# Two cross-attention layers: the transposed probabilities of each pair of heads leave PSUM head by head, half by ScalarE and half by VectorE, ahead of the row maxima

## What is computed

```python
def _gqa_forward(hidden_state, encoder_hidden_state, encoder_attention_mask, Wq, bq, Wk, bk, Wv, bv, Wo, bo, gamma, beta):
    ...
    scores = jnp.einsum('bkgld,bksd->bkgls', q, k) * scale
    scores = scores + encoder_attention_mask[:, :, None, :, :]
    attn = jax.nn.softmax(scores, axis=-1)
    out = jnp.einsum('bkgls,bksd->bkgld', attn, v)
...
def _L1_xattn_ref(hidden_states, audio_kv, audio_attention_mask, Wq, Wk, Wv, Wo, ln_gamma, ln_beta, gate):
    ...
    a = _layer_norm(audio_kv, ln_gamma, ln_beta)
    ...
    attn = jax.nn.softmax(scores, axis=-1)
    out = jnp.einsum('bhts,bhsd->bhtd', attn, V)
    out = out.transpose(0, 2, 1, 3).reshape(B, Tt, D)
    out = out @ Wo.T
    return hidden_states + jnp.tanh(gate) * out
```

## Time and profile before

| what | value |
|---|---|
| median of 3 runs | 1238.89 us (1238.04 to 1239.21) |
| the profiled execution's own time | 1238.88 us |
| its span, first to last instruction | 1237.1 us |
| PE busy | 1163.7 us (94%) |
| DVE busy | 810.3 us (65%) |
| ACT busy | 749.9 us (61%) |
| POOL busy | 259.9 us (21%) |
| granted TensorE clock, mean | 0.991 |

### The profile page before, as it was taken

The page is one execution under the profiler, slowest core; times in us unless marked ns, Lnnn a source line. Parts: engine busy times, 40 slices in busy tenths (PEclk is TensorE's granted clock), DMA queues, the critical chain, the costliest instruction groups (busy, mean ns, idle before and its releaser), DMA issues.

```text
span 1237.1 us, 32215 instructions
## 1 busy us (share of the span) xinstructions
PE 1163.7 (94%) x9987; PEld 942.3 (76%) x9987; DVE 810.3 (65%) x2387; ACT 749.9 (61%) x2163; POOL 259.9 (21%) x280
## 2 busy tenths in 40 slices
PE   4899999999999999999999999999999999999997
PEld 4678787777878777787877778777787877778785
DVE  4465667667576775757667575766757576676734
ACT  3374756747475674747567474856747476574744
POOL 2042213121131312113121121312112131212210
PEclk9799999999999999999999999999999999999999
DMA  7674536447353654736365472635637263563600
GB/s 240 180 175 99 143 88 157 117 100 189 81 156 76 147 134 91 193 75 156 86 135 146 88 195 68 163 88 123 158 88 181 71 162 98 110 167 81 149 11 8
DMA packets 77821, 153.77 MB, mean 124 GB/s; under 512 B 10384, under 2 KB 47056, under 8 KB 77152
## 3 DMA queue, kind: packets, MB, share of 16 engines
q1 hardware_dynamic: 77792, 153.40, 50.6%
HBM read 113.72 MB, written 39.65 MB: 124 GB/s over the span
## 4 chain that ended last, share of the span: by engine, by line
PE 72%; issue 12%; DVE 9%; ACT 4%; DMA 1%; DVEq 1%; POOL 1%; ACTq 0%; SPq 0%; POOLq 0%
PE PJ L365 17%; PE TP L416 13%; PE SCO L402 6%; PE OA L436 5%; PE SCO L460 5%; PE SCO L681 5%; PE PJ L378 5%; PE PJ L468 4%; DVE SCO L819 3%; PE SCO L406 3%; PE SCO L365 2%; ACT PR L1049 2%; DVE PT L829 2%; DVE MN L819 1%; PE SCO L666 1%
## 5 line engine op out<-in xcount | busy, mean ns | idle before, releaser
L1049 ACT ACTIVATE PR<-SCO,MN 100x361 f32<-100x361 f32 x768 | 424.8, 564 | 154.3 <-DVE MN L819 151.1
L819 DVE CUSTOM_DVE_ANT_0 SCO<-SCO,MK 100x361 f32<-100x361 f32 x768 | 402.3, 549 | 148.1 <-PE SCO L402 102.3
L416 PE MATMUL TP<-ident,PR 100*128 100x100 f32 x2304 | 268.4, 252 | 22.3 <-DVE PT L829 19.7
L416 PEld LDWEIGHTS TP<-ident,PR 100*128 100x128 f32 x2304 | 226.9, 141 | 80.5 <-DVE PT L829 27.1
L1060 ACT ACTIVATE PT<-TP 121x600 f32<-121x600 f32 x256 | 173.0, 676 | 77.0 <-PE TP L416 76.6
L402 PE MATMUL SCO<-K0S,Q0S 128*100 128x362 f32 x512 | 164.1, 375 | 19.7 <-ACT PR L1049 17.5
L1049 ACT ACTIVATION_READ_ACCUMULATOR PR<-SCO,MN 100x1 f32 x768 | 158.2, 206 | 0.0
L829 DVE COPY PT<-TP 121x600 f32<-121x600 f32 x128 | 100.0, 781 | 52.1 <-PE TP L416 50.1
L819 DVE DVE_READ_ACCUMULATOR2_ANT MN<- 100x1 f32 x768 | 108.7, 141 | 0.0
L402 PEld LDWEIGHTS SCO<-K0S,Q0S 128*100 128x100 f32 x512 | 75.4, 166 | 43.1 <-ACT PR L1049 38.2
L406 PE MATMUL SCO<-K1S,Q1S 128*100 128x362 f32 x256 | 96.6, 387 | 8.1 <-ACT Q1S L1171 5.0
(11 more groups left out here) (142 smaller groups left out, 1827.7 us busy)
## 6 DMA issues: line engine op xcount, KB each, us to landing
K1S<-k_scr SPq DMA_DIRECT2D x128, 364.0 KB, 6.1
k_scr<-K1HL SPq DMA_DIRECT2D x64, 364.0 KB, 2.5
Q0S<-q_scr SPq DMA_DIRECT2D x128, 100.0 KB, 3.9
K0S<-k_scr SPq DMA_DIRECT2D x64, 182.0 KB, 4.8
AT<-ctx_cols SPq DMA_DIRECT2D x16, 722.0 KB, 9.3
V<-ctx_rows SPq DMA_DIRECT2D x16, 484.0 KB
q_scr<-QHL SPq DMA_DIRECT2D x16, 400.0 KB, 2.5
k_scr<-K1HL SPq DMA_DIRECT2D x32, 182.0 KB, 3.1
```

What stands on the lines that cost most here:

```text
L416: last = pe.transpose(TP[:, k % 2, c * T:(c + 1) * T], PR[0:T, k % NPR, c * SP:c * SP + P], ident[0:T, 0:T])
L819: dve.tensor_tensor_reduce(out=bank, in0=bank, in1=mask[0:T, :], scale=scale, scalar=3.4e38, op0=ALU.add, op1=ALU.min, accum_out=MN[0:T, k ...
L1049: act.activation(PR[0:T, k % NPR, 0:S], SCO[0:T, k % 3, 0:S], ACT.Exp, bias=MN[0:T, k:k + 1], scale=-1.0, accum_out=SM[0:T, k:k + 1]).then ...
```

## The change

Every pair is now copied by both engines at once: ACT copies the bank of its first head (121 x 300), DVE the bank of its second head (121 x 300). PE increments `pt_mm` after each head, so ACT can start after three transposes. PE waits for ACT's copy of the pair before ahead of the first head's transposes, and for DVE's ahead of the second head's. The exps wait for their slot of PR by heads and no longer by pairs. On DVE the copy of pair p-3 now stands ahead of both row maxima of step p in every step of L0 and L1. Pairs 14 and 15 are copied on DVE around the sums of the batch's second unit of 16 heads (`repeat_sums(b, 1)`).

```diff
             def transpose_probs(b, p):
                 pe.wait_ge(prob, NH * b + 2 * p + 2)
-                if p > 0:
-                    pe.wait_ge(*copied_out(b, p - 1))
-                elif not isinstance(b, int) or b > 0:
-                    pe.wait_ge(*copied_out(b - 1, NPAIR - 1))
+                wait_from(pe, pt_act, NPAIR * b + p)
                 for k in (2 * p, 2 * p + 1):
+                    if k % 2 == 1:
+                        wait_from(pe, pt_dve, NPAIR * b + p)
                     for c in range(SC):
                         last = pe.transpose(TP[:, k % 2, c * T:(c + 1) * T], PR[0:T, k % NPR, c * SP:c * SP + P],
                                             ident[0:T, 0:T])
-                last.then_inc(pt_mm, 1)
+                    last.then_inc(pt_mm, 1)
...
             def probs_out(b, p):
-                dve.wait_ge(pt_mm, NPAIR * b + p + 1)
+                dve.wait_ge(pt_mm, NH * b + 2 * p + 2)
...
-                dve.tensor_copy(PT[0:SP, h % 2, 2 * (p % 4):2 * (p % 4) + 2, :], TP[0:SP, :, 0:SC * T]).then_inc(pt_dve, 1)
+                dve.tensor_copy(PT[0:SP, h % 2, 2 * (p % 4) + 1, :], TP[0:SP, 1, 0:SC * T]).then_inc(pt_dve, 1)
...
                 for p in range(L0P):
-                    if p % 4 == 0 and (p > 0 or not first):
-                        if p > 0:
-                            probs_out(b, p - 3)
-                        else:
-                            probs_out(b - 1, NPAIR - 3)
-                    elif p == 2 and not first:
-                        probs_out(b - 1, NPAIR - 1)
+                    if p >= 3:
+                        probs_out(b, p - 3)
+                    elif not first:
+                        probs_out(b - 1, NPAIR - 3 + p)
...
+                probs_out(b, 14)
                 repeat_sums(b, 1)
+                probs_out(b, 15)
...
                 for p in range(L0P, NPAIR):
+                    if p >= 19:
+                        probs_out(b, p - 3)
                     shift(b, 2 * p)
-                    if p in (20, 22):
-                        probs_out(b, p - 3)
-                    elif more and p == 18:
+                    if more and p == 18:
...
             def exps(b, k):
                 act.wait_ge(shifted, NH * b + k + 1)
-                wait_from(act, pt_mm, NPAIR * b + k // 2 - 2)
+                wait_from(act, pt_mm, NH * b + k - 5)
...
             def probs_out(b, p):
-                act.wait_ge(pt_mm, NPAIR * b + p + 1)
+                act.wait_ge(pt_mm, NH * b + 2 * p + 1)
...
-                act.activation(PT[0:SP, h % 2, 2 * (p % 4):2 * (p % 4) + 2, :], TP[0:SP, :, 0:SC * T], ACT.Copy).then_inc(pt_act, 1)
+                act.activation(PT[0:SP, h % 2, 2 * (p % 4), :], TP[0:SP, 0, 0:SC * T], ACT.Copy).then_inc(pt_act, 1)
...
-                    if p >= 3 and (p - 3) % 4 != 1:
+                    if p >= 3:
                         probs_out(b, p - 3)
-                    elif p == 1 and not first:
-                        probs_out(b - 1, NPAIR - 2)
+                    elif not first:
+                        probs_out(b - 1, NPAIR - 3 + p)
...
                     exps(b, 2 * p - 2)
-                    if p in (19, 21, 23):
+                    if p >= 19:
                         probs_out(b, p - 3)
                     exps(b, 2 * p - 1)
```

More of the change, by code:

```diff
@@ L40, in two_layer_cross_attention @@
     NPAIR, L0P = NH // 2, 16
-    ACT_OUTS, DVE_OUTS = 16, 8
     NPR = 6
@@ L192, in two_layer_cross_attention @@
         REP_BANK = (SCO[:, 2, 0:C * T], TP[:, 0, 0:C * T], TP[:, 1, 0:C * T], SCO[:, 0, 0:C * T])
[L194 to L202, removed]
         def head0(k):
@@ L425, in out_half @@
                     if part == 0:
-                        pe.wait_ge(pt_act, ACT_OUTS * b + (3 * h + 3 if h < 4 else 2 * h + 6))
-                        pe.wait_ge(pt_dve, DVE_OUTS * b + (h + 1 if h < 4 else 2 * h - 2))
+                        pe.wait_ge(pt_act, NPAIR * b + 4 * h + 4)
+                        pe.wait_ge(pt_dve, NPAIR * b + 4 * h + 4)
                         if h % 2 == 0:
@@ L822, in probs_out @@
             def probs_out(b, p):
-                dve.wait_ge(pt_mm, NPAIR * b + p + 1)
+                dve.wait_ge(pt_mm, NH * b + 2 * p + 2)
                 h = p // 4
-                if p == 5 and isinstance(b, int) and b == 0:
+                if p == 4 and isinstance(b, int) and b == 0:
                     dve.wait_ge(v1w_l, 1)
-                if p % 4 == 1:
+                if p % 4 == 0:
                     wait_from(dve, pv, NHALF * b + h - 1)
-                dve.tensor_copy(PT[0:SP, h % 2, 2 * (p % 4):2 * (p % 4) + 2, :], TP[0:SP, :, 0:SC * T]).then_inc(pt_dve, 1)
+                dve.tensor_copy(PT[0:SP, h % 2, 2 * (p % 4) + 1, :], TP[0:SP, 1, 0:SC * T]).then_inc(pt_dve, 1)
             def repeat_sums(b, u):
@@ L1017, in _ @@
             batch(NB - 1, False, False)
-            probs_out(NB - 1, NPAIR - 3)
+            for p in (NPAIR - 3, NPAIR - 2):
+                probs_out(NB - 1, p)
             repeat_sums(NB - 1, 2)
@@ L1193, in _ @@
             exps(NB - 1, NH - 1)
-            probs_out(NB - 1, NPAIR - 2)
+            for p in range(NPAIR - 3, NPAIR):
+                probs_out(NB - 1, p)
             unit_sums(NB - 1, 2, C * T)
```

## The result

The changed kernel takes 1249.26 us (median of 4 runs, 1248.49 to 1249.88), the kernel before 1238.64 in the same comparison (1238.04 to 1239.21). The ratio is 1.0083, with a 95% interval of 1.0071 to 1.0096: it is slower by 0.8%, where 1206 was forecast. Yet nearly everything that the forecast named for the profile is there.

What follows compares the result with a forecast made beforehand. PE's order of work was taken as the path, with its waits for DVE and ACT winnable. 2.0 us a batch over 14 batches (28.0), plus 1.7 and 3.2, made 33: 1238.9 - 33 = 1206 us, range 1197 to 1226.

Steps and rivals of the forecast that it cites:

- the signs named as showing it wrong: Transposes' halves over 0.3 us apart unstalled, exp waits all over L1, PE idle at keys after L1, half copies near 0.5.
- the idle time with DVE's copy as releaser: PE's idle time before the transposes, waiting for DVE's copy, was to fall from 46.8 us to under 15.
- L1, steps 20 to 23: DVE's copy ahead of the row maximum lets PE's transposes start earlier: 0.72 + 0.95 = 1.67 us won a batch.
- The ring of banks: Three score banks in L1 allow 1.32 us a pair, 0.17 under PE's 1.49, so it barely holds.
- L0, steps 0 to 4: DVE's whole copies at steps 0, 2 and 4 each become 0.31 shorter ahead of the maxima: 0.93 us won a batch.
- L0, steps 9 to 11: New DVE copies among gated result, sums and statistics delay PE: -0.75 us, back to -0.6 with ACT's earlier half at step 15.
- Batches 0 and 15 and the end: Gains outside the loop: 1.7 us in batch 0 (L1 part alone), 3.2 in batch 15 with its very end.
- The second wait: PE's wait between a pair's two heads was put at 0; it could show one weight load, 141 ns.
- The end of L0: DVE's wait for pairs 14 and 15 delays the context split, still done 0.3 us before PE asks: nothing lost.
- Rival A: DVE's load eats half the gain in L1 and steps 9 to 11: 1.0 us a batch, 1223 (1215 to 1231); chance 0.25.
- Rival C: No change, 1239: PE's waits move from copies to exps because the ring of banks was the true limit; chance 0.06.
- Rival D: Smaller waits at steps 18, 21 and 23 of L1 go too, 0.5 us a batch more: 1198 or less; chance 0.07.

Runs made afterwards that it cites:

- with one wait: Changed kernel without 96 semaphore increments on DVE, both waits of a pair put ahead of the first head's transposes: 1197.16 us, against 1195.36 with the wait between the heads.
- the kernels without the stall: Changed kernel without 96 semaphore increments on DVE (48 ahead of its loop): 1195.36 us; changed kernel with 60 one-byte memsets ahead of DVE's loop: 1196.76 us.
- order alone: Kernel before, whole copies, with DVE's copy in steps 20 and 22 ahead of both row maxima instead of between them: 1221.26 us (0.9857).
- halves alone: Changed kernel without 96 semaphore increments on DVE, half copies kept, DVE's copy in L1 put back between the two row maxima: 1218.57 us (0.9837).
- the kernel before with 16 fills: Kernel before with 16 one-byte memsets added on DVE ahead of its loop, which then lies at records 277 to 576: 1306.31 us (1.0533).
- with 40: Kernel before with 40 one-byte memsets added on DVE ahead of its loop, which then lies at records 300 to 599: 1333.51 us (1.0772).

## Why the prediction was wrong, point by point

**The step that failed.** The sum of the parts took the copies added on VectorE (16 a batch, with which its loop has ten records more) at the time that each takes and nothing else ("Sum: 1.67 + 0.93 - 0.6 = 2.0 us a batch, for 14 batches of the loop 28.0"). What it lacked is a term for the loop's code. The loop went from records 260 to 559 to records 276 to 585, over the point between 559 and 576 that the end of a loop with such a start may not pass. Each of 13 jumps back then stalls DVE, for 3.35 us in the one shown. With the same loop body at another place the time is 1196.76, so the term is 1249.26 - 1196.76 = 52.5 us, 4.0 a jump. With 42.0 won this gives 1238.6 - 42.0 + 52.5 = 1249.1; measured 1249.3. No rival had it, and none of the signs named as showing it wrong appeared. Two of the signs named as showing it right stayed away: the idle time with DVE's copy as releaser was 41.8 us instead of under 15, and a batch took 74.5 us instead of 70.8.

The sign in the trace of before was the count of records and the 13 packets of the instruction queue; I read neither. That the 4.0 us are the idle time (L0 60.7 instead of 57.9 in the batches where the clock stayed up) and the lower clock behind it (62.3 where it fell) is read from the stages, not tried by itself. The stages add up: three jumps at 2.8 and ten at 4.4 are 52.4 us, against 52.5.

**L1, steps 20 to 23: 1.67 us forecast, 1.83 measured** (14.07 to 12.24). Right in place and cause. The ring of banks held with its thin margin: pairs 1.43 to 1.52 apart.

**L0, steps 0 to 4: 0.93 forecast.** The waits for exps at the start of a batch (0.29, 0.22 and 0.36 us of idle time 3, 7 and 11 us into it) are gone. What PE takes in steps 0 to 6 beyond the shortest time between the same operations fell by 1.26 us.

**L0, steps 9 to 11: -0.6 forecast.** Right: two waits of 0.48 and 0.26 us appear, one step later than named (steps 11 and 12; the prediction has 10 and 11). By the same count as above, steps 11 and 12 take 0.64 us more, and step 15 takes 0.18 less: -0.46.

L0 in all: 0.33 forecast, 0.80 measured (58.69 to 57.89), so a batch gains 2.6 us instead of 2.0: the mechanisms were right and the sum 0.6 too small: 0.33 in the early steps, 0.16 in L1, 0.14 in the late steps. Batches 0 and 15 and the end were put at 4.9; 42.0 - 14 x 2.62 = 5.3.

**The second wait: 0.** Right as far as shown: with one wait the kernel is not faster.

**The end of L0: 0.** Right: L0 got shorter by what the early steps gave.

**Rival A** (DVE's load eats half) was wrong: the copies gained more than forecast. The Trainium skill's rule on small tiles (VectorE: DVE Perf Modes, the section on the errata), weighed in the prediction, had the price nearly right (438 ns an estimate, 468 measured), and little of it reached the path: the 0.64 us of steps 11 and 12. **Rival C** was wrong too: L1 fell by 1.83 us, so the ring of banks was not the limit there. **Rival D** (1198 or less) has the time of the kernels without the stall, 1195.4 and 1196.8, but not their mechanism: it wanted 0.5 us a batch more in L1, and L1 gave 0.16 more, the early steps of L0 0.33.

## What to carry to other kernels

Where a kernel runs in a hardware loop, count each engine's instructions in it and where it lies in the program, before and after a change: a stall for "issue" right behind the jump back, and the packets of the instruction queue (12 to 14 against 78 here), show whether it fits. A kernel that gets some per cent slower or faster for no reason that its work shows may only have moved. Runs with different numbers of idle instructions ahead of the loop tell: one is not enough, since here 60 removed the stall and 20 and 130 did not. Here such a move hid a gain of 3.4%. And a copy for which PE waits is to be both short and ahead of what waits itself: order alone gave 1.01 us of L1, halves alone 0.28, both 1.83.

## What the runs showed that I had not expected

- The same loop body costs 1196.76 or 1248.65 us by whether 60 or 20 idle instructions stand ahead of it.
- A stall of 3.35 us on DVE costs 4.0 us a jump in the changed kernel, 5.2 in the kernel before with 16 fills ((1306.3 - 1239.0) / 13) and 7.3 with 40, where the fetch stalls twice. In the changed kernel the granted clock falls behind 10 of the 13 jumps.
- Transfers of q14 come in pieces of 8 KB. The Trainium skill (Advanced Engine Details and Errata, "ISA Cache") speaks of 32 KB with lines of 16 KB, two of them, and says that this can be configured for each engine. Two lines of 256 instructions and four of 128 hold the same. That a loop of 299 to 315 fits at some places and not at others agrees with both. But the size of the packets and the distance of the points at which they are ordered, 117 to 129 records, are those of the smaller piece. So is the distance of the two points that a loop's end may not pass: one lies between 559 and 576, the next between 645 and 715, so they are 69 to 156 records apart.
